# Perceiver block on one core: attention, time mixing, routing and first experts in one program block, with tokens listed chunk by chunk

## The reference

```python
x = x + xattn(layernorm(x), ctx, ctx, ...)      # keys: 257 context tokens of the sequence, then its own 32
x = x + attn(layernorm(x), ...)                 # time mixing, then experts
x = x + ffn(layernorm(x), ...)                  # shared GeGLU and one of 8 expert GeGLUs

# attn:
xn = ln(x, ln1_g, ln1_b); xx = shift(xn)        # shift: the token before, zero for the first
k, v, r = mix(xn, xx, mu_k) @ Wk, mix(.., mu_v) @ Wv, sigmoid(mix(.., mu_r) @ Wr)
x = x + r * wkv(k, v, time_decay, time_first) @ Wo     # a scan over the 32 tokens
ei = ln(x, ln2_g, ln2_b)
vals, idx = top_k(softmax(ei @ router_w), 2); wts = vals / vals.sum()
xk_e = ei * mk[e] + shift(ei) * (1 - mk[e]); xr_e likewise
expert = sigmoid(xr_e @ eWr[e]) * (square(relu(xk_e @ eWk[e])) @ eWv[e])
x = x + sum over the two experts of wts * expert
```

## Time and profile before

| | us |
|---|---|
| median of 3 runs | 1023.5 (1023.16 to 1024.01) |
| the profiled execution | 1025.3 |
| its span | 1023.6 |
| TensorE busy (matmul records) | 893.4 |
| VectorE, ScalarE, GpSimd busy | 438.7, 291.2, 279.8 |
| mean granted clock of TensorE | 0.943 of full |

### The profile page before, as it was taken

The page is one execution under the profiler, slowest core; times in us unless marked ns, Lnnn a source line. Parts: engine busy times, 40 slices in busy tenths (PEclk is TensorE's granted clock), DMA queues, the critical chain, the costliest instruction groups (busy, mean ns, idle before and its releaser), DMA issues. The chain is left out here.

```text
span 1023.6 us, 19906 instructions
## 1 busy us (share of the span) xinstructions
PE 893.4 (87%) x6694; PEld 809.5 (79%) x6695; DVE 438.7 (43%) x1126; ACT 291.2 (28%) x648; POOL 279.8 (27%) x520
## 2 busy tenths in 40 slices
PE   6899987889850499999995999995899999999995
PEld 4566657888840399999994999995799999999994
DVE  2354445999956455555552333335211111111113
ACT  1333324666620254554441111110011111111110
POOL 1664442444443232232203222220210010010006
PEclk8999998999965599999997999997999999999998
DMA  9887828511110242222212111010588988899715
GB/s 348 290 291 276 303 83 285 147 42 32 33 39 4 93 161 86 80 79 87 77 51 63 32 42 37 31 31 27 196 315 331 321 300 327 305 317 326 276 58 164
DMA packets 97918, 163.40 MB, mean 160 GB/s; under 512 B 10136, under 2 KB 76184, under 8 KB 95672
## 3 DMA queue, kind: packets, MB, share of 16 engines
q1 hardware_dynamic: 85552, 120.84, 34.4%
q0 software_dynamic: 6528, 19.54, 7.0%
q10 hardware_dynamic: 5776, 22.22, 5.4%
HBM read 146.06 MB, written 16.52 MB: 159 GB/s over the span
## 5 line engine op out<-in xcount | busy, mean ns | idle before, releaser
L1306 PEld LDWEIGHTS bank<-zT_f,we 128*128 128x128 f32 x1472 | 167.8, 192 | 3.3 <-issue 1.5
L1306 PE MATMUL bank<-zT_f,we 128*128 128x128 f32 x1472 | 168.3, 275 | 1.6 <-issue 1.1
L1323 DVE TENSOR_TENSOR hT_f<-bank,act_g 128x512 f32<-128x512 f32 x78 | 53.8, 691 | 230.4 <-PE bank L1306 217.1
L1315 ACT ACTIVATE act_g<-bank 128x512 f32<-128x512 f32 x78 | 46.6, 597 | 323.7 <-PE bank L1306 323.7
L1306 PE MATMUL bank<-zT_c,a_x 128*128 128x128 f32 x1024 | 122.7, 283 | 0.3 <-PEq L978 0.3
L1306 PEld LDWEIGHTS bank<-zT_c,a_x 128*128 128x128 f32 x1024 | 120.5, 199 | 0.8 <-issue 0.7
L726 PE MATMUL bank<-xn,mixed_w 128*128 128x128 f32 x768 | 94.0, 280 | 1.3 <-ACT xn L808 0.9
L726 PEld LDWEIGHTS bank<-xn,mixed_w 128*128 128x128 f32 x768 | 90.0, 195 | 2.3 <-ACT xn L808 1.3
L1330 PE MATMUL bank<-we,hT_f 128*128 128x256 f32 x368 | 83.3, 380 | 0.0
L1183 PE MATMUL bank<-xk,wk_e 128*128 128x128 f32 x624 | 78.0, 280 | 0.2
L1183 PEld LDWEIGHTS bank<-xk,wk_e 128*128 128x128 f32 x624 | 74.5, 196 | 0.9 <-DVE xr L1237 0.5
(11 more groups left out here) (227 smaller groups left out, 1286.7 us busy)
## 6 DMA issues: line engine op xcount, KB each, us to landing
we<-in_W_dram SPq DMA_DIRECT2D x69, 1024.0 KB, 7.3
ctx_sb<-in_ctx_n_dram ACTq DMA_DIRECT2D x16, 1152.0 KB, 7.4
kT<-in_ctx_t_dram SPq DMA_DIRECT2D x16, 1028.0 KB, 8.9
rows_y<-y SPq DMA_DIRECT2D x39, 128.0 KB, 1.7
ewk_sb<-in_eWk_dram SPq DMA_DIRECT2D x1, 4096.0 KB, 14.2
ewv_sb<-in_eWv_dram SPq DMA_DIRECT2D x1, 4096.0 KB
rows_f<-yr ACTq DMA_DIRECT2D x23, 128.0 KB, 6.2
ewr_sb<-in_eWr_dram SPq DMA_DIRECT2D x1, 2048.0 KB, 19.8
```

What stands on the lines that cost most here:

```text
L1306: last = nc.tensor.matmul(bank[half][:, f * P:(f + 1) * P], w12[:, i, k, col0:col0 + P], zT[:, k], start=k == 0, stop=k == KD - 1)
L1315: nc.scalar.activation(act_g[:, half], bU[half][:], ACT.Gelu).then_inc(self.ac_g, 1)
L1323: nc.vector.tensor_tensor(hT[:, parity, half * HH:(half + 1) * HH].rearrange("p f t -> p (f t)"), bG[half][:], act_g[:, half], ALU.mult).t ...
```

## The change

Attention, time mixing, routing and first experts become one block with one set of semaphores. Their tiles are cut from two arenas in SBUF, which the stages use one after the other, so that the first use of a place or a PSUM bank waits for its last user.

- Each engine runs attention steps 0 to 17 and time mixing steps 0 to 21; from attention step 15 on, a mixing step follows each attention step. The barriers and the clearing of semaphores between the stages go; one of each stands behind the experts.
- Time mixing: `rw` moves to GpSimd (`quotient`), the logits are copied by ScalarE, the bias of the router comes by a matmul with a row of ones, `bb` lies in the PSUM bank `bB`, `dk` is one instruction.
- Routing: in steps behind each chunk's logits VectorE takes its top 2, the one-hot masks and, after TensorE's rank matmuls, the place of each token within its expert; GpSimd keeps the running count and stores the token numbers to the DRAM table `tab_e` with two indirect DMAs a chunk. Each expert has room for 16 tiles in `tab_e`, which is zeroed first. A chain `tile_map` at the end makes `expert1` and `place1` (where in `tab_e` a tile lies). Softmax is replaced by a sigmoid of the difference of the two logits, in the expert loop.
- First experts: SyncE loads each tile's 128 token numbers from `tab_e` to `pick`, at a place that it reads from `place1`. The three 1 MB loads go out at tiles 18 to 20. GpSimd adds x1 and a_x2 a chunk at a time in tiles 2 to 17. The mixing weights `cm_mu` come with the constants `late`, not by 16 DMAs.

The diff, cut to its core:

```diff
-LATE = 2 * 8 + 6 + 12 + 2 + 2 * 256
+LATE = 2 * 8 + 6 + 12 + 32 + 2 * 256
...
+        ATT_STEPS = G + 2
+        MIX_STEPS = G + 6
+        MIX_AT = G - 1
...
+        def mix_sync(sp):
+            sp.wait_ge(po_mix, 1)
+            sp.dma_start(rows_e.rearrange("(b s) d -> b s d", s=S)[:, 0, 0:D], zero_rows[:]).then_inc(zero_out, 16)
+            sp.dma_start(tab_e.rearrange("(p f) o -> p (f o)", p=P), zero_tab[:]).then_inc(zero_tab_out, 16)
+            sp.wait_ge(dv_x1, G)
...
+            def quotient(n):
+                pool.wait_ge(dv_rec, n + 1)
+                need(pool, pe_x, n - 1)
+                pool.drain()
+                nc.gpsimd.tensor_tensor(rw[:, n % 2], num[:, n % 2], den[:, n % 2], ALU.mult).then_inc(po_rw, 1)
+
+            def count(n):
+                pool.wait_ge(dv_mask, n + 1)
+                need(pool, pe_rank, n)
+                need(pool, po_sum, n)
+                nc.gpsimd.tensor_tensor(earlier[:, (n + 1) % 2], earlier[:, n % 2], mask[:, n % 2], ALU.add).then_inc(po_sum, 1)
+
+            def list_tokens(n):
+                if n == 0:
+                    pool.wait_ge(zero_tab_out, 16)
+                pool.wait_ge(dv_slot, n + 1)
+                for k in range(2):
+                    nc.gpsimd.indirect_dma_start(out=tab_e[:, :],
+                                                 out_offset=bass.IndirectOffsetOnAxis(ap=listed[:, n, k:k + 1], axis=0),
+                                                 in_=token[:, n:n + 1], in_offset=None).then_inc(po_tab, 16)
+
+            def step(s):
+                w, g, h, i = live(s - 2), live(s - 4), live(s - 5), live(s - 6)
...
+                if g is not None:
+                    rstd3(g)
+                if w is not None:
+                    numerator(w)
+                if i is not None:
+                    list_tokens(i)
+                if g is not None:
+                    normed(g)
+                if h is not None:
+                    count(h)
+                if w is not None:
+                    quotient(w)
...
+            def ranks(n):
...
+                nc.tensor.matmul(bX[:, D:D + E], before_m[:], mask[:, n % 2], start=True, stop=False)
+                nc.tensor.matmul(bX[:, D:D + E], ones_m[:], earlier[:, n % 2], start=False, stop=True).then_inc(pe_rank, 1)
...
+        def moe_sync(sp):
+            def load_pick(s):
+                at = sp.value_load(place1[0:1, bass.ds(s.n, 1)], min_val=0, max_val=T_ROWS // P - 1)
+                sp.dma_start(pick[:, s.slot], tab_e[bass.ds(at * P, P), :]).then_inc(m_pick[s.slot], 16)
+            sp.wait_ge(dv_map, 1)
+            sp.wait_ge(po_tab, 2 * G * 16)
+            for i in range(NM):
+                load_pick(Step(0, i, NM))
+
+            def body(s):
+                ahead = s.back(-NM, NT1)
+                if ahead:
+                    sp.wait_ge(m_pa, s.n + 1)
+                    load_pick(ahead)
+                if isinstance(s.n, int) and s.n in (18, 19):
+                    sp.wait_ge(m_x12, G)
+                    i = s.n - 18
+                    sp.dma_start(ws12[:, i], (w1s, w2s)[i].rearrange("(k p) h -> p k h", p=P)).then_inc(ld_s, 16)
+                if isinstance(s.n, int) and s.n == 20:
+                    sp.dma_start(ws3, w3s.rearrange("(f p) d -> p f d", p=P)).then_inc(ld_s, 16)
+                sp.wait_ge(m_dy, s.n + 1)
+                sp.dma_start(rows_y[bass.ds(s.n * P, P), :], y[:, s.slot]).then_inc(m_put[s.slot], 16)
+            sweep(sp, NT1, 21, NM, body, NM)
...
+        def moe_pool(pool):
...
+            def body(s):
+                e = pool.value_load(expert1[0:1, bass.ds(s.n, 1)], min_val=0, max_val=E - 1)
+                need(pool, m_dx, s.n - NM + 1)
+                pool.wait_ge(m_pick[s.slot], s.lap * 16 + 16)
+                nc.gpsimd.tensor_copy(mu_e[:, s.slot], cm_mu[:, :, e]).then_inc(m_mu, 1)
+                nc.gpsimd.indirect_dma_start(out=pair[:, s.slot], out_offset=None, in_=rows_e[:, :],
+                                             in_offset=bass.IndirectOffsetOnAxis(ap=pick[:, s.slot], axis=0)
+                                             ).then_inc(m_got[s.slot], 16)
...
+            @block.tensor
+            def _(pe):
+                att, mix = att_tensor(pe), mix_tensor(pe)
+                for s in range(ATT_STEPS):
+                    att(s)
+                    if s >= MIX_AT:
+                        mix(s - MIX_AT)
+                for s in range(ATT_STEPS - MIX_AT, MIX_STEPS):
+                    mix(s)
+                moe_tensor(pe)
```

More of the change, by code:

```diff
@@ L163, in perceiver_block @@
         g1, b1, wd, u_c, g2_c, b2_c = (late[:, 22 + 2 * i:24 + 2 * i] for i in range(6))
-        g2, b2 = (late[:, 36 + D * i:36 + D * (i + 1)] for i in range(2))
+        cm_mu = late[:, 34:34 + 2 * E * KD].rearrange("p (i e k) -> p i e k", i=2, k=KD)
+        g2, b2 = (late[:, 66 + D * i:66 + D * (i + 1)] for i in range(2))
         wexp = sb("wexp", [P, KD])
@@ new lines, in perceiver_block @@
+        logits = sb("logits", [P, G, E])
+        top = sb("top", [P, G, 8])
+        top_at = sb("top_at", [P, 2, 8], U32)
+        hot = sb("hot", [P, G, 2, E])
+        listed = sb("listed", [P, G, 2], U32)
+        moved = sb("moved", [P, E])
+        moved_k = sb("moved_k", [P, G, 2])
+        mask = sb("mask", [P, 2, E], BF16)
+        earlier = sb("earlier", [P, 2, E], BF16)
+        hot_rank = sb("hot_rank", [P, 2, E])
+        rank = sb("rank", [P, 2])
+        token = sb("token", [P, G], I32)
@@ new lines, in perceiver_block @@
+        N3 = 3
+        in_a = Carve(arena_a, FLOATS_A)
+        w_T = in_a.take(4, KD, D)
+        early = in_a.take(EARLY)
+        bq_c, bk_c = early[:, 0:KD], early[:, KD:2 * KD]
+        bv_b, bo_b = early[:, 4:4 + D], early[:, 4 + D:4 + 2 * D]
+        ctx_sb = in_a.take(N3, BG * TC * D + D)
+        kT = [in_a.take(BG, KD, KW) for _ in range(N3)]
+        hn, v_own, o_nat = (in_a.take(2, D) for _ in range(3))
+        hnT, qT, oT = (in_a.take(2, KD, P) for _ in range(3))
+        prob = in_a.take(2, KW)
@@ new lines, in perceiver_block @@
+        probT = in_a.take(2, 3, P)
+        lora_sb = Carve(arena_b, FLOATS_B).take(8, D)[0:R]
+        in_b = Carve(arena_b, FLOATS_B)
+        z_in = in_b.take(2, D)
+        xn = [in_b.take(KD, BG, SP1) for _ in range(2)]
+        pp, dk, e1b, e2b, e_in, evb, num, den, rw = (in_b.take(2, D) for _ in range(9))
+        aa = in_b.take(2, D)
+        z3, ei = in_b.take(2, D), in_b.take(2, D)
+        zT3 = in_b.take(2, KD, P)
+        NM = 3
+        in_a = Carve(arena_a, FLOATS_A)
+        ewk_sb = in_a.take(E, KD * FK)
@@ new lines, in perceiver_block @@
+        ewv_sb = in_a.take(E, FKC * D)
+        ewr_sb = in_a.take(E, KD * D)
+        in_b = Carve(arena_b, FLOATS_B)
+        cmp_eg = in_b.take(E, G)
+        cmp_te = in_b.take(NT1, E)
+        hot_moved = in_a.take(G * 2, E)
+        in_b = Carve(arena_b, FLOATS_B)
+        pair = in_b.take(NM, 2 * D)
+        wk_e = in_b.take(NM, KD * FK)
+        prevT, diffT, xk, xr = (in_b.take(NM, KD * P) for _ in range(4))
+        sig, y = in_b.take(NM, D), in_b.take(NM, D)
+        h_relu = sb("h_relu", [P, NM, FK], F32, moe_scope)
@@ L1269, in perceiver_block @@
[L1269 removed]
+        moe_scope.close()
         KEPT = 4
```

1763 lines of the change are left out of this document (917 added, 846 removed).

## The result

| | before | after |
|---|---|---|
| median of runs | 1023.75 us (4 runs, 1023.16 to 1025.45) | 1189.24 us (4 runs, 1183.6 to 1195.83) |
| ratio, 95% interval | | 1.162 (1.154 to 1.169) |
| profiled execution, its span | 1025.3, 1023.6 | 1193.6, 1191.9 |
| TensorE busy, mean granted clock | 893.4, 0.943 | 957.7, 0.892 |

What follows compares the result with a forecast made beforehand. It saw a VectorE-bound time mixing stage, a hole at the routing, then an expert loop with no slack on TensorE. Terms -8 + 1 - 26 + 48 + 4 + 1 = +20 gave 1045, or 1043 us against the median; range 1017 to 1070.

Steps and rivals of the forecast that it cites:

- Border: Attention to time mixing: mixing step 0 behind attention step 15 brings the first running maximum earlier; -8 us, bounds -4 and -12.
- Steps of mixing: Time mixing: VectorE stays about equal, GpSimd with stores and drains comes level with the step; +1 us, bounds -5 and +11.
- Tail: Last logits to first expert tile: the new routing chain ends at 321.5 in place of 347.7; -26 us, bounds -20 and -31.
- Loop: Expert loop: index load queued behind the wait for y, round trip L of 7.57 us; +48 us, bounds +42 and +78.
- rival (b): Expert loop: the clock falls to the 1.2 GHz level, +157 us in place of 48, 1150 in all; chance 0.05.
- (d): The forecast itself, all terms as summed, 1043 us against the median; chance 0.70.
- 1 MB loads: Expert loop: weight loads at tiles 18 to 20, just behind an index load, slow three gathers; +4 us, bounds 0 to 8.
- Semaphores: One clearing of some hundred semaphores in place of two smaller; +1 us, bounds 0 to 2.
- (a): Expert loop: the index load is early enough or parts overlap; with no stall at all 992 us; chance 0.14.
- (c): Mixing and tail: GpSimd becomes mixing's bound, stores costing 2 us each, not 1.25; +18 us, 1061 in all; chance 0.11.

Runs made afterwards that it cites:

- e8: The kernel before with one GpSimd drain right behind each gather of the expert loop; one run, 1055.7 us.
- e15: After, with mixing's GpSimd drains as waits on own semaphores, y stored two bodies later and 64-byte list rows, all written; 1002.1 us, ratio 0.980 to before.
- e13: After, drains kept, token list with 64 bytes a row, each store still writing 4 bytes; one run, 1113.6 us.
- e14: After, drains kept, token list with 64 bytes a row, each store writing the whole row; one run, 1099.5 us.
- e4: After, with SyncE storing y of tile n-2 in the body that loads the indices of tile n+3; 1087.1 us, ratio 1.061 to before.

## Why the prediction was right and wrong

**Border, -8: right at its first maximum (-6.1, within its bounds), wrong one step later.** The first product came at 154.97, not near 152.5, and not at full clock (0.55 in 150 to 157 us). What failed is "Attention step 17 is now in between, 1.6 us of TensorE and 1.5 of VectorE": it was priced by its work, but the first step became 6.0 us longer by its place, as the trace reads: most of that is VectorE's wait of 5.17 us for its product. No run moved it.

**Steps of mixing, +1 (to +11): wrong, +65.4.** The step that failed is "With 0.6 of drains GpSimd comes to 7.9 us". I priced the added drains as VectorE's flushes of 0.15 and the stores by their issue, and issue was right (1.02 and 0.25 between, for 1.25). A drain behind an indirect DMA waits for its landing: 3.3 us behind one gather (e8), 6.8 on the mean behind these stores (94.6 in 14 times). The trace of before had gathers followed by a drain, but only in front of the next tile's gather, some 4 us after the start of one that lands in 3.3, so its row (0.86 of idle) could not show the rule. I also left out TensorE's own additions. The groups of e15, 210 to 270 us, seven steps, show them:

```profile
L831 PE MATMUL bank<-b_row,ones_row 1*128 1x8 f32 x14 | 2.7, 262 | 0.0
L841 PE MATMUL bank<-mask,before_m 128*128 128x8 bf16 x7 | 1.3, 180 | 1.7 <-DVE mask L1017 1.7
L842 PE MATMUL bank<-earlier,ones_m 128*128 128x8 bf16 x7 | 1.2, 167 | 0.0
```

That is 5.2 / 7 = 0.74 us a step on an engine that was at 44.1 of 48.7. They do not account for all of the 10.1 us that e15's mixing is longer than before's: 6.0 are the first step (12.03 for 6.07), 3.4 the last nine (8.49 a step for 8.11), 0.8 the rest. For the 0.38 a step of the last nine TensorE's additions are my reading; no run took them out alone.

**Tail, -26: wrong for after, +4.5.** In e15, another kernel, the chain is about as forecast: its tail is 39.7, 25.8 us shorter than before. The steps that failed: two stores in a tail step cost their drain on top, 4.8 to 6.7 us in four steps, 23.7 in all, and "the second lands 3.3 after its start, as a gather does": in after the last store starts at 395.04 and SyncE, which waits for the list, issues the first index load at 405.19. Less 1.1 for the register read, that is 9 us. In e15 the same is 313.54 to 318.77, 4 us. The Trainium skill (DMA: Bandwidth & Descriptors, Anatomy of one DMA) says that a DMA's semaphore can only count once the target memory has confirmed the last byte; the trace agrees: the last store's packets are over 2.0 us after its start, its last increment comes after 9.1. (The 2.0 us that the prediction takes for any DMA is that section's figure for those that GpSimd issues; SyncE's index loads landed in 2.0 on the median of after.) Its Specifications warn of read-modify-write below 512 bytes; here 4 and 64 bytes, both below, waited alike (20.6 and 20.9 us in e13 and e14), so the size alone is not what cost.

**Loop, +48 (42 to 78): mechanism right, size wrong, +103.5.** Two things were mis-sized. One is L: 8.92 in place of 7.57. The register read with its wait took 1.11 in place of 0.65, the index load 2.19 in place of 1.8, copy to gather 0.66 in place of 0.34, gather to transposes 3.75 in place of 3.35. With it (8.92 + 4.82)/2 - 4.82 = 2.05 a tile, 35 x 2.05 = 72, and 67 us of added waits were measured. The other is the clock, which the term put at full: its 37 us I had only as rival (b), all or nothing, while the granted clock was 0.79 on the mean of 380 to 620, between the two levels' 0.5 and 1.0, with TensorE busy 163 of the 240 us. That it had kept full clock once in 6 us with 4.4 busy was too little to build on. e4 shows the two belong together: without the waits both go. The forecast should have merged (d) with a part of (b).

**1 MB loads, +4:** e4's loop, with the loads at tiles 18 to 20, is 0.9 longer than before's, so there they cost 1 us or nothing; in after no run takes them apart. **Semaphores, +1:** the rest of the span is +1.0, but it lies between -3.1 and +3.7 in the other kernels, so this term is not shown.

**Rivals.** (a), slack in the round trip, fell. (c) named the right engine and stage for the wrong reason, the issue of stores in place of what a drain makes of them, and at 18 us was 47 short in mixing alone. None named the slow landing of the stores.

## What to carry to other kernels

Price a store by when it has landed, not by its issue, and ask of each barrier behind it (a drain, a semaphore) which of the two it waits for; for an engine's own order use its own semaphore. A list written element by element from many partitions wants its entries apart in memory (here 64 bytes). Where a queue carries both a result out and an input in, put the input's load ahead of the wait for the result: an edit of a few lines gave back 102 us. And price a merged border at the second step too: a gain at the first instruction can be lost in the engines' order behind it.

## What was unexpected of the hardware

- A GpSimd drain waits until indirect DMAs issued before it have landed; what stands behind it starts 0.1 us (e8) or 0.2 us (after, e13, e14) after the last increment. The wait was 3.3 us behind one gather, 5 to 11 behind two 4-byte stores into a dense table, 1.5 on the mean (20.9 us in 14 times) behind stores into 64-byte rows.
- Dense 4-byte writes landed slowly (8.2 us on the mean for the second of two, 2.9 with 64 bytes between), and other DMA was slow beside them: without drains, row packets that took 0.05 us took up to 8, and instruction fetches, 5 to 7 in each window, 1.4 to 2.8 us on the mean in place of 0.8. That neighbouring writes wait for each other in one piece of memory is my explanation of e13; which part of the memory does it, and how far apart is enough between 4 and 64 bytes, was not tried.
- With the drains kept, the loop was shorter in e13 and e14 (277 and 265 us) than in after (285) although nothing in the loop's order changed. Single runs, with a granted clock of 0.84 and 0.86 in 330 to 530 us, and index loads that landed in 1.7 us on the median in place of 2.0; left open.
